# Pairwise attention pooling on one core: one phase of transposes and Gram matrices per four steps, and x scaled by GpSimd

## The reference

```python
row, col = np.triu_indices(F, k=1)                 # x: (2048, 39, 64), 741 pairs
ip = x[:, row, :] * x[:, col, :]
hidden = relu(einsum('bpd,da->bpa', ip, W_w) + b_w)      # D = A = 64
logits = einsum('bpa,a->bp', hidden, W_h) + b_h[0]
a = softmax(logits, axis=1)[:, :, None]
pooled = sum(a * ip, axis=1)
y = pooled @ W_p + b_p
```

## Time and profile before

| | us |
|---|---|
| median of 3 runs | 1133.52 (1133.19 to 1134.34) |
| the profiled execution, its own time | 1133.69 |
| its span in the profile | 1130.9 |
| TensorE busy | 1104.3 |
| VectorE busy | 991.4 |
| ScalarE busy | 880.9 |
| GpSimd busy | 304.6 |
| granted TensorE clock, mean of the span | 0.996 of full speed |

### The profile page before, as it was taken

How to read it: one execution, slowest core, us unless ns; L and a number is a source line. 1 busy time by engine, 2 the same in 40 slices (tenths; PEclk the granted TensorE clock), 3 DMA queues, 4 the chain that set the end, 5 groups by cost and what they waited for, 6 DMA issues and landing times.

```text
span 1130.9 us, 61839 instructions
## 1 busy us (share of the span) xinstructions
PE 1104.3 (98%) x25856; PEld 515.5 (46%) x25856; DVE 991.4 (88%) x741; ACT 880.9 (78%) x929; POOL 304.6 (27%) x263
## 2 busy tenths in 40 slices
PE   6999999999999999999999999999999999999995
PEld 2444444444444444444444444444444444444442
DVE  7989989898898988989889898898989889898891
ACT  3878787787877778787777877877777787877884
POOL 2512214132141412314222141321414114141330
PEclk9999999999999999999999999999999999999998
DMA  2223242321323223132232313213222232321412
GB/s 43 39 43 43 36 47 39 43 40 34 51 38 46 39 36 47 34 52 38 35 50 37 46 34 45 44 34 49 39 37 44 40 46 37 52 36 34 48 25 23
DMA packets 341661, 45.80 MB, mean 40 GB/s; under 512 B 341600, under 2 KB 341600, under 8 KB 341600
## 3 DMA queue, kind: packets, MB, share of 16 engines
q1 hardware_dynamic: 340672, 45.20, 26.8%
q10 hardware_dynamic: 928, 0.00, 0.0%
HBM read 26.59 MB, written 18.54 MB: 40 GB/s over the span
## 4 chain that ended last, share of the span: by engine, by line
PE 95%; ACT 3%; issue 1%; SPq 0%; DVE 0%; DMA 0%; ACTq 0%; DVEq 0%
PE z L438 58%; PE logits L458 29%; PE cross L413 5%; PE cross L402 4%; ACT hidden L349 2%; ACT exps L357 1%; DMA x_rows<-in_r_x_dram 0%; SPq L178 0%; SPq L149 0%; DVE neg_max L278 0%; DVE weighted L287 0%; ACT x_scaled L342 0%; PE logits L448 0%; ACTq L348 0%; DVE x_wide L251 0%
## 5 line engine op out<-in xcount | busy, mean ns | idle before, releaser
L349 ACT ACTIVATE hidden<-z,b_col 128x988 f32<-128x988 f32 x768 | 819.0, 1084 | 224.1 <-PE z L438 223.6
L265 DVE TENSOR_TENSOR prod<-x_wide 128x2964 f32<-128x2964 f32 (+1 forms) x257 | 826.6, 3232 | 37.4 <-PE z L438 37.3
L438 PE MATMUL z<-prod,w_tiles 64*32 64x494 f32 x12288 | 790.4, 580 | 3.3 <-issue 2.2
L226 POOL COPY head_w<-head_cols 128x64 f32<-128x64 f32 x252 | 299.5, 1196 | 794.4 <-PE logits L458 794.4
L458 PE MATMUL logits<-hidden,head_w 64*32 64x371 f32 (+1 forms) x8192 | 437.1, 472 | 4.8 <-ACT hidden L349 3.2
L438 PEld LDWEIGHTS z<-prod,w_tiles 64*32 64x32 f32 x12288 | 236.9, 106 | 238.8 <-issue 117.6
L458 PEld LDWEIGHTS logits<-hidden,head_w 64*32 64x32 f32 x8192 | 180.6, 106 | 239.3 <-issue 234.3
L402 PEld LDWEIGHTS cross<-ident,x_rows 39*128 39x128 f32 x1024 | 42.2, 140 | 109.9 <-issue 109.9
L250 DVE COPY x_wide<-cross 128x312 f32<-128x312 f32 x128 | 61.4, 480 | 32.9 <-PE cross L413 30.4
L342 ACT ACTIVATE x_scaled<-x_wide,wp_col 128x312 f32<-128x312 f32 x128 | 70.2, 549 | 6.2 <-DVE x_wide L251 5.3
L413 PE MATMUL cross<-x_wide,x_scaled 64*39 64x39 f32 x4096 | 65.3, 204 | 0.0
(11 more groups left out here) (15 smaller groups left out, 18.2 us busy)
## 6 DMA issues: line engine op xcount, KB each, us to landing
x_rows<-in_r_x_dram SPq DMA_DIRECT2D x256, 78.0 KB
gram<-gram_out SPq DMA_DIRECT2D x512, 23.8 KB
gram<-gram_out SPq DMA_DIRECT2D x512, 11.6 KB
values<-gram SPq DMA_DIRECT2D x128, 46.3 KB, 3.4
out_dram<-y_all SPq DMA_DIRECT2D x8, 1.0 KB, 2.5
w_tiles<-in_L_rec_W_w_dram SPq DMA_DIRECT2D x4, 16.0 KB, 2.2
head_cols<-in_L_rec_W_h_dram ACTq DMA_DIRECT2D x4, 0.2 KB, 2.4
wp_col<-in_L_rec_W_p_dram ACTq DMA_DIRECT2D x2, 0.2 KB, 2.4
```

The source lines that it names most:

```text
L226: nc.gpsimd.tensor_copy(head_w[:, step % AHEAD, :, :], head_cols[:, :, at:at + TILE]).then_inc(head_w_ready, 1)
L265: nc.vector.tensor_tensor(out, one, other, ALU.mult).then_inc(ready, 1)
L349: nc.scalar.activation(hidden[:, e, :, CHUNK * k:CHUNK * (k + 1)], z[:, (THIRDS * e + k) % 2, :, 0:CHUNK], ACT.Relu, bias=b_col[:, 0:1]).t ...
L438: last = nc.tensor.matmul(z[col:col + TILE, (THIRDS * e + k) % 2, b, 0:CHUNK], w_tiles[row:row + D, col:col + TILE], prod[row:row + D, e, ...
```

## The change

A **block** of four steps takes the place of the unit. There is one cross phase per block, with 16 transposes and 64 Gram matmul instructions. The transposes go to a PSUM tensor of their own (`x_cols`, the same size as `cross`). The Gram matrices of a block become a 13th item in z's ring of two slots, between chunks 5 and 6 of the block's 12, so every chunk behind it moves one slot on (`item`). ScalarE, which reads the ring anyway, copies them out (`copy_gram`), with the exponentials of an ended group ahead of that copy. VectorE spreads a whole block at once, after the block's four multiplies; it takes a group's maximum ahead of that spread and pools the group behind the next block's first multiply. GpSimd scales x of a whole block in one instruction (`scale_x`) ahead of the block's four `head_w` copies, into one buffer where there were two. Only the first block's second half is spread by ScalarE. SyncE issues one set of 2 loads and 8 Gram writes per block, each twice as large; of the 8 stores of y ScalarE issues four.

```diff
-                for m in range(GROUP_UNITS):
-                    unit = GROUP_UNITS * g + m
-                    if not (last and m >= GROUP_UNITS - 4):
-                        sp.wait_ge(cross_ready, unit + 3)
-                        load(unit + 4, m % SLOTS)
...
+                for m in range(GROUP_BLOCKS):
+                    v = GROUP_BLOCKS * g + m
+                    if not (last and m >= GROUP_BLOCKS - 2):
+                        sp.wait_ge(x_cols_ready, v + 2)
+                        load(v + 2, m % SLOTS)
...
+            def scale_x(v):
+
+                pool.wait_ge(x_spread, 2 * (v + 1))
+                if v == 0:
+                    pool.wait_ge(act_spread, 2)
+                    pool.wait_ge(cols_loaded, 16 * N_COLS)
+                else:
+                    pool.wait_ge(z_ready, ITEMS * (v - 1) + CROSS_AT + 1)
+                nc.gpsimd.tensor_scalar(x_scaled[:, :, :], x_wide[:, v % SLOTS, :, 0:FIELDS], wp_col[:, 0:1], None,
+                                        ALU.mult).then_inc(x_scaled_ready, 1)
+
+            scale_x(0)
             pool.wait_ge(head_cols_loaded, 16 * 4)
...
+            for step in range(BLOCK_STEPS, STEPS):
+                if step % BLOCK_STEPS == 0:
+                    scale_x(step // BLOCK_STEPS)
                 place_heads(step)
...
-                multiply(2 * unit, unit, slot, 0)
-                if not (isinstance(unit, int) and unit + 1 >= UNITS):
-                    spread(unit + 1, 1 - slot)
-                copy_gram(unit - 1, 1 - slot, earlier)
-                if ended is not None:
-                    pool_group(ended, parity, loads)
-                multiply(2 * unit + 1, unit, slot, 1)
...
+                multiply(v, slot, 0)
+                if pooled_group is not None:
+                    pool_group(*pooled_group)
+                for i in range(1, BLOCK_STEPS):
+                    multiply(v, slot, i)
                 if ended is not None:
                     find_max(ended)
+                if more:
+                    spread(v + 1, 1 - slot)
...
-            def scale_x(unit, slot):
-                act.wait_ge(x_spread, 2 * (unit + 1))
-                nc.scalar.mul(x_scaled[:, slot, :, :], x_wide[:, slot, :, 0:FIELDS],
-                              wp_col[:, 0:1]).then_inc(x_scaled_ready, 1)
...
+            def copy_gram(v, slot, writes):
+
+                act.wait_ge(z_ready, ITEMS * v + CROSS_AT + 1)
+                if not (isinstance(writes, int) and writes == 0):
+                    act.wait_ge(gram_written[slot], 16 * GRAM_DMAS * writes)
+                nc.scalar.copy(gram_out[0:ROWS, slot, :, :, :],
+                               z[0:ROWS, (slot + CROSS_AT) % 2, :, 0:XCOLS].rearrange("p u (d f) -> p u d f", f=FIELDS)
+                               ).then_inc(z_read, 1)
...
+            def block_work(v, slot, writes, ended=None):
+
+                for j in range(CHUNKS):
+                    rectify(v, slot, j)
+                    if j == CROSS_AT - 1:
+                        if ended is not None:
                             exponentials(ended)
+                        copy_gram(v, slot, writes)
...
+            def gram_matrices(v, slot):
+                pe.wait_ge(x_scaled_ready, v + 1)
+                pe.wait_ge(z_read, ITEMS * v + CROSS_AT - 1)
                 nc.tensor.sem_inc(z_claimed, 1)
...
+            def cross_work(v, slot, loads=None):
+
+                if loads is not None:
+                    pe.wait_ge(x_spread, 2 * (v + 1))
+                    pe.wait_ge(x_loaded[1 - slot], 32 * loads)
+                    nc.tensor.sem_inc(z_claimed, 1)
+                    transpose(1 - slot, range(2))
+                gram_matrices(v, slot)
...
+                first_half(v, 0)
+                chunks(7)
+                second_half(v, 0)
+                chunks(8, 9)
+                first_half(v, 1)
+                chunks(10)
+                second_half(v, 1)
+                chunks(11, 0)
+                first_half(v, 2)
+                chunks(1)
+                second_half(v, 2)
+                chunks(2, 3)
+                first_half(v, 3)
+                chunks(4)
+                second_half(v, 3)
+                chunks(5)
                 if following:
+                    cross_work(v + 1, 1 - slot, loads)
+                chunks(6)
```

More of the change, by code:

```diff
@@ L294, in pool_group, with block_work @@
                                         ALU.mult, ALU.add).then_inc(y_ready, 1)
-            def unit_work(unit, slot, earlier, ended=None, parity=0, loads=0):
+            def block_work(v, slot, pooled_group=None, ended=None, more=True):
+                multiply(v, slot, 0)
[3 more added lines that the diff above has]
+                    multiply(v, slot, i)
                 if ended is not None:
@@ L310, in _ @@
-            multiply(0, 0, 0, 0, slice(1, QUADS, 2))
-            multiply(1, 0, 0, 1)
-            spread(1, 1)
-            multiply(2, 1, 1, 0)
-            spread(2, 0)
-            copy_gram(0, 0, 0)
-            multiply(3, 1, 1, 1)
-            unit_work(2, 0, 0)
-            def group(g, parity, loads):
-                for m in range(3, GROUP_UNITS + 3):
-                    unit, earlier = GROUP_UNITS * g + m, GROUP_UNITS // 2 * g + (m - 1) // 2
-                    if m == GROUP_UNITS + 2:
-                        unit_work(unit, m % SLOTS, earlier, ended=g, parity=parity, loads=loads)
-                    else:
-                        unit_work(unit, m % SLOTS, earlier)
@@ new lines, in _ @@
+            spread(0, 0, first=True)
+            multiply(0, 0, 0, slice(0, QUADS, 2), first_prod_ready)
+            multiply(0, 0, 0, slice(1, QUADS, 2))
+            for i in range(1, BLOCK_STEPS):
+                multiply(0, 0, i)
+            spread(1, 1)
+            group(0)
+            with dve.Fori(0, (GROUPS - 2) // 2) as k:
+                group(2 * k + 1, (2 * k, 0, k + 1))
+                group(2 * k + 2, (2 * k + 1, 1, k + 1))
+            block_work(BLOCKS - 3, 1, pooled_group=(GROUPS - 2, 0, GROUPS // 2))
@@ L406, in gram_matrices @@
-            def gram_matrices(unit, slot):
-                pe.wait_ge(x_scaled_ready, unit + 1)
-                nc.tensor.sem_inc(z_claimed, 1)
-                for duo in (j * QUADS + p for p in range(QUADS) for j in range(2)):
-                    j, p = duo // QUADS, duo % QUADS
-                    for h in range(2):
-                        row, col = h * D, (h ^ j) * D
-                        last = nc.tensor.matmul(
-                            cross[col:col + FIELDS, j, GCOLS.start + p * FIELDS:GCOLS.start + (p + 1) * FIELDS],
-                            x_scaled[row:row + D, slot, duo, :], x_wide[row:row + D, slot, duo, 0:FIELDS],
-                            start=True, stop=True, tile_position=(row, col))
-                return last
@@ L419, in cross_work, with transpose @@
[L419 to L427 removed]
+            def transpose(slot, tiles):
+                for d in range(ROW_DUOS):
+                    for u in tiles:
+                        rows = slice(u * D, u * D + FIELDS)
+                        duo = x_rows[rows, slot, 2 * d:2 * d + 2, :].rearrange("f h d -> f (h d)")
+                        last = nc.tensor.matmul(x_cols[:, u, FIELDS * d:FIELDS * (d + 1)], duo, ident[rows, :],
+                                                is_transpose=True, start=True, stop=True, tile_position=(u * D, 0))
+                last.then_inc(x_cols_ready, 1)
@@ new lines, in gram_matrices @@
+            def gram_matrices(v, slot):
+                pe.wait_ge(x_scaled_ready, v + 1)
+                pe.wait_ge(z_read, ITEMS * v + CROSS_AT - 1)
+                nc.tensor.sem_inc(z_claimed, 1)
+                at = (slot + CROSS_AT) % 2
+                for d in range(ROW_DUOS):
+                    for u in range(2):
+                        for h in range(2):
+                            row, col, duo = h * D, (h ^ u) * D, u * ROW_DUOS + d
+                            last = nc.tensor.matmul(z[col:col + FIELDS, at, u, FIELDS * d:FIELDS * (d + 1)],
+                                                    x_scaled[row:row + D, duo, :],
+                                                    x_wide[row:row + D, slot, duo, 0:FIELDS],
+                                                    start=True, stop=True, tile_position=(row, col))
+                last.then_inc(z_ready, 1)
```

320 lines of the change are left out of this document (145 added, 175 removed).

## The result

The changed kernel takes 1335.13 us (median of 4 runs, 1334.71 to 1337.37) against 1133.89 us: a ratio of 1.178, 95% interval 1.176 to 1.180. The forecast was 1117.3. The profiled execution spans 1335.4 us. First the page of the changed kernel: busy shares, the queue of instruction packets, the chain that ended last, and three groups.

The account below looks back on a forecast made before the run. TensorE, busy 98% of the span, was taken as the bound. The terms -22.9 + 5.6 + 3.9 - 3.0 + 0 = -16.4 on 1133.69 us gave about 1117.3, with a range from about 1108 to 1132.

Parts of the forecast that it names:

- Part 1: TensorE's cross phase, one per block: a doubled phase takes 1.59 us against 1.96 for two, -22.9 us in all.
- Part 2: Gram matrices in z's ring: one more chunk stall per block, +5.6 us, and later logits at group ends, +3.9.
- Part 2's pairs: Three places per block with two adjacent chunks, each waiting 0.09 us for a ring slot; before there were two.
- the group end: Boundary between groups on TensorE: 0.50 us extra before, +0.24 more in 15 groups, +3.9 us with rounding.
- Part 3: VectorE: doubled spread 0.82 and 0.47 us, multiplies 3.15 each, 13.85 of a 16.84 us block; gains nothing by itself.
- Part 4: Scaling on GpSimd: takes 0.9 us, mostly waits for the fourth multiply, hidden with 3.0 us there: 0.
- one of the signs: Multiplies on VectorE waiting for GpSimd, listed among what would show the forecast wrong.
- rival (c): Multiplies and GpSimd's instructions exclude each other; scaling takes 2.85 us, VectorE plus GpSimd bounds: +48, 1181 us; chance 0.12.
- rival (b): Scaling slower than taken but under 3.6 us delays the Gram matrices: +14, 1131 us, no change; chance 0.06.
- Prologue: Start: Gram matrices at 19.1 us after scaling, logits open at 21 instead of 24.23: -3.0 us.
- The end: After the loops: later values +1.7 us, output on two queues -1.9, together 0 (-1.9 to +2).
- The output on two queues: End of the kernel: eight output issues take 3.76 us on one queue; on two, -1.9 us.

Follow-up runs that it names:

- e1: The changed kernel with TensorE's outer loop begun at the start of a 256-instruction fetch block (slot 0): 1144.49 us, ratio 1.010.
- e2: As e1, but the loop begun at slot 160 of a fetch block, so that eight blocks are touched again: 1307.49 us, ratio 1.153.
- e12: The changed kernel at its own alignment, with a prefetch hint for the way back of TensorE's outer loop: 1157.12 us, ratio 1.021.
- e9: As e1, but SyncE issues the load of block v+2's x only when block v's third multiply is done: 1133.98 us, ratio 1.0005.
- e10: As e9, but GpSimd scales every block's x twice, once into a spare tile: 1137.09 us.
- e4: The changed kernel with both of TensorE's loops unrolled, no branch back: 1313.03 us, ratio 1.158.
- e6: As e1, but each load of x from block 3 on fetches 2 of 16 batches (wrong results): 1133.7 us, ratio 1.000.
- e7: As e1, but Gram writes in the group loop store one of eight pairs, values loaded from the first group's (wrong results): 1133.17 us, ratio 1.000.

## Why the prediction was wrong

**The step that failed** stands in none of the parts: `two_blocks`, the doubled body of TensorE's inner loop, was costed at nothing and not named. I listed what instructions cost, never how many there are. The text's own rule out, "The change failing to do what it says is no case: all its phases are written out", was where a rival on the length of the code belonged. Its price was 190.6 us (e1) and would have turned the forecast round. The earlier trace rows had the length: 25856 matmuls and as many loads, 51712 in 64 blocks, 808 a block. What fits was in no row; it took e1, e2 and e12.

**Part 1 was right.** In e9 the phase is 519.05 less 518.05 (1.00, of which 0.83 are the chunk's), 0.62 and 0.84: 1.63 for 1.59. **Part 2's pairs** cost 0.08 each (514.22 to 515.98 is 1.76, less 1.68) for 0.09, and chunk 7 follows 6 after 1.45, without a wait. The clean block takes 16.87 for 16.84; the group end adds 0.77 (68.25 less four blocks) where 0.50 + 0.24 were counted. The forecast's sum makes a group 68.06 (68.92 less 4 x 0.28, plus 0.26; the 3.9 for 15 ends is 0.24 each, rounded up from 3.6): over 14 groups 2.7 us.

**Part 2 left out** what the larger transfers do. Its queue of SyncE wasn't followed: a load of x right behind the Gram writes cost 10.5 us (e1 less e9). Only issue times at the end were read.

**Part 3** was near: the spread takes 0.80 and 0.46 us (0.82, 0.47). The multiplies start 3.34 us apart, not 3.15: in the block shown one of four takes 3.75, the others 3.25 to 3.28.

**Part 4 was right in its cost, wrong in how it comes about.** The scaling was hidden, with room for another (e10). But it did not wait for the fourth multiply: it becomes ready with the first (521.07) and is done 4.9 us later, 1.6 behind the first one's end. And the multiply that stands behind it takes 0.50 longer: multiplies do wait for GpSimd, one of the signs that the prediction named for being wrong, but once a block and inside VectorE's idle time. So rival (c)'s mechanism is there at 0.50 us in place of 2.85, and its 1181 did not happen. Nor did rival (b)'s wait of the Gram matrices.

**Prologue:** the opening at 21.3 us in e9 is as forecast, by luck: the first scaling was done at 17.4, the Gram matrices started at 17.52 and not at 19.1, and 2.0 us on issue made up for it. In the changed kernel the logits open at 19.18. The first group of e9 then takes 73.1 us for 68.9 before (94.39 less 21.29): the doubled body is fetched for the first time within it. Stalls of 0.89 and 0.77 us on issue show, and 3.4 us at the lower clock; the rest wasn't followed. **The end** was forecast at 0 and costs 8.6 (81.5 us from the last opening to the end, 72.9 before). Rows of e9:

```profile
1085.53 0.42 PE L444 MATMUL z<-x_wide,x_scaled 64*39 64x39 f32 x21 [0.89 <-issue]
...
1103.85 0.51 PE L444 MATMUL z<-x_wide,x_scaled 64*39 64x39 f32 x32 [1.68 <-issue]
...
1116.23 0.93 DVE L296 TENSOR_REDUCE neg_max<-logits 128x1 f32<-128x742 f32 x1 [17.55 <-PE logits L493]
...
1121.64 0.93 DVE L305 CUSTOM_DVE_ANT_0 weighted<-exps,values 128x742 f32<-128x742 f32 x1 [4.17 <-DMA values<-gram]
...
1123.06 1.80 SPq L158 DMA_DIRECT2D out_dram<-y_all  x4
```

TensorE's last group is 4.8 longer (66.4 for 61.6 from opening to maximum): 2.8 of it are waits on issue, where code behind the loops is met for the first time (the kernel before has none there, with code as new); the other 2.0 weren't followed. The pooling follows the maximum after 5.4 us instead of 2.3, +3.1 for the +1.7 taken. The output on two queues brings 0.7 us more, not 1.9 less: issues end earlier, but from the first issue to the end it is 8.3 us for 7.6.

Together, in spans: the forecast's is 1130.9 - 16.4 = 1114.5; + 2.7 (groups) + 5.0 (first group, 68.06 in the sum) + 9.2 (end, with the 0.6 that the sum took off its two blocks) + 0.1 (opening) = 1131.5, and e9's is 1131.4. That execution's own time is 1133.17, the median 1133.98. The collision adds 10.5 (e1), and the refetch 190.6: 1335.1.

## What to carry to other kernels

Count the instructions that a loop holds on each engine, not only their time: here each fp32 matmul is four, and a doubled body that removes work cost 18%, because a pass touched eight blocks of 256 where seven stay. Look at the instruction queue's packets in the page first when an engine waits on "issue"; if they grow with the loop's passes, shorten the body, set the loop's start (1144.5 us here) or hint its way back (1157.1). And when transfers are merged into fewer and larger ones, follow the queue that issues them: two that lay apart can then be in flight together.

## What the runs showed of the hardware

- TensorE kept a loop of 7 blocks of 256 instructions and refetched one of 8, at the same length (e1: 19 packets, e2: 146). With a hint at the way back it kept 8 (e12: 19).
- A miss at the way back stands for 3.3 to 3.5 us, twice in a row (changed kernel, 513 and 517 us); and the granted clock is at 1.2 GHz for 6.8 us from there (514.35 to 521.17).
- Straight-line code is not free: unrolled, TensorE lost over 100 us to issue (e4).
- Two transfers that are harmless apart delay the news of a finished chunk by up to 1.3 us when in flight together (e1, e6, e7, e9). The matmuls behind it start on time, so reading their inputs is not what is held up; whether writing the result or the semaphore is stays open.
- A scaling on GpSimd gets in behind one multiply of VectorE, and the next multiply takes 3.75 us instead of 3.25 (e9; with two scalings two of them, e10). The Trainium skill (SBUF — State Buffer, SBUF: two separate sides) has one block the other for a whole instruction, whichever starts first. The trace agrees for the scaling, which waits out the first multiply; the next multiply waits 0.5 us of the 1.6 that the scaling still takes, so for it "whole" is not shown.
